# Expert rows scaled by the gate and added to the output by accumulating indirect DMA, without a combining stage

## The reference

```python
h = layernorm(x) @ Wr1 + br1;  h = gelu(layernorm(h) * ln_scale + ln_bias)
p = softmax(h @ Wr2 + br2);  top2, idx = top_k(p, 2);  gate = top2 / sum(top2)
for e in range(8):
    x1, x2 = split(layernorm(x) @ W1[e] + b1[e])       # 128 -> 2 x 512
    y = (x1 * gelu(x2)) @ W2[e] + b2[e]                # 512 -> 128
    output += y * gate_of(e)                            # 0 where e is not among the two
return x + output
```

## Time and profile before

| | us |
|---|---|
| median of three runs | 1981.48 (1976.96 to 1983.18) |
| the profiled execution | 1981.65 |
| its span, first to last instruction | 1979.9 |

### The profile page before, as it was taken

How to read it: one execution, slowest core, us unless ns; L and a number is a source line. 1 busy time by engine, 2 the same in 40 slices (tenths; PEclk the granted TensorE clock), 3 DMA queues, 4 the chain that set the end, 5 groups by cost and what they waited for, 6 DMA issues and landing times. The chain is left out here.

```text
span 1979.9 us, 50794 instructions
## 1 busy us (share of the span) xinstructions
PE 1674.4 (85%) x12709; PEld 1283.0 (65%) x12710; DVE 1455.8 (74%) x5309; ACT 1068.1 (54%) x2080; POOL 1091.8 (55%) x2255
## 2 busy tenths in 40 slices
PE   3599999999999999999999999835444699999990
PEld 1366766766766766766766766634434599999990
DVE  4588788788788788788778788736555577777775
ACT  2067666666666666666666666501111465656553
POOL 4047546547547547547547547416877455555650
PEclk8599999999999999999999999955555799999995
DMA  4436436426426427327426426274221211111119
GB/s 167 127 95 155 107 85 159 110 77 164 112 70 172 111 64 177 109 64 174 109 71 167 109 81 165 75 236 116 65 65 42 67 53 52 51 53 53 52 49 257
DMA packets 167897, 212.14 MB, mean 107 GB/s; under 512 B 28049, under 2 KB 129313, under 8 KB 167681
## 3 DMA queue, kind: packets, MB, share of 16 engines
q1 hardware_dynamic: 137216, 149.63, 27.2%
q0 software_dynamic: 30464, 59.96, 12.2%
HBM read 127.01 MB, written 77.22 MB: 103 GB/s over the span
## 5 line engine op out<-in xcount | busy, mean ns | idle before, releaser
L778 DVE CUSTOM_DVE_ANT_0 junk<-pA,lmask 128x512 bf16<-128x512 f32 x1056 | 688.2, 683 | 224.5 <-PE pA L489 114.6
L720 ACT ACTIVATE prob<-pB 128x512 f32<-128x512 f32 x512 | 305.6, 597 | 194.0 <-PE pB L510 162.9
L722 ACT ACTIVATE prob<-pB 128x512 f32<-128x512 f32 x512 | 305.2, 596 | 1.3 <-PE pB L512 1.1
L489 PE MATMUL pA<-K,QL 96*128 96x512 f32 (+3 forms) x792 | 286.1, 363 | 19.9 <-DMA K<-split_operands 14.3
L528 PE MATMUL pC<-prob,vext 128*32 128x256 f32 x4112 | 283.8, 393 | 2.9 <-POOL prob L403 2.9
L403 POOL TENSOR_TENSOR prob<-prob,upper_diag 128x128 f32<-128x128 f32 x512 | 255.0, 498 | 47.8 <-POOL prob L398 10.5
L512 PE MATMUL pB<-QL,K 97*128 97x512 f32 (+3 forms) x768 | 279.4, 364 | 0.0
L510 PE MATMUL pB<-QU,K 97*128 97x512 f32 (+3 forms) x640 | 269.7, 421 | 7.4 <-ACT prob L720 2.8
L491 PE MATMUL pA<-K,QU 96*128 96x512 f32 (+3 forms) x660 | 235.9, 359 | 12.1 <-DVE acc L778 7.2
L396 POOL MEMSET prob<- 1x1 f32 x448 | 39.5, 88 | 345.6 <-ACT prob L722 345.5
L1471 POOL DMA_INDIRECT expert_rows<-yb,dst x144 | 158.2, 1098 | 102.5 <-DVE yb L1592 74.5
(11 more groups left out here) (272 smaller groups left out, 3437.7 us busy)
## 6 DMA issues: line engine op xcount, KB each, us to landing
QL<-split_operands SPq DMA_DIRECT2D x67, 256.0 KB, 3.5
QU<-split_operands SPq DMA_DIRECT2D x67, 256.0 KB, 3.9
K<-split_operands SPq DMA_DIRECT2D x67, 256.0 KB, 3.9
xg<-routed_rows SPq DMA_DIRECT2D x76, 130.0 KB
QL<-split_operands SPq DMA_DIRECT2D x67, 128.0 KB, 3.5
QU<-split_operands SPq DMA_DIRECT2D x67, 128.0 KB, 3.7
K<-split_operands SPq DMA_DIRECT2D x67, 128.0 KB, 3.7
split_operands<-c_h POOLq DMA_DIRECT2D x16, 512.0 KB, 6.4
```

Of the source, the lines that this page charges most:

```text
L489: mm = pe.matmul(dst[:, 0:low], QL[0:KROWS, s, q], K[0:KROWS, s, k0:k0 + low], start=True, stop=True)
L720: act.activation(p[:, 0:HALF], pB[:, 0:HALF], ACT.Exp, scale=SCALE).then_inc(p_exp, 1)
L722: act.activation(p[:, HALF:S], pB[:, HALF:S], ACT.Exp, scale=SCALE).then_inc(p_exp, 1)
L778: v.tensor_tensor_reduce(junk[:, n % S1_BUFS, :], pA[n % S1_BUFS][:, :], lmask[:, at:at + HALF], 1.0, -3.0e38, ALU.add, ALU.max, acc[:, s, ...
```

## The change

- A row in `xs` has two more floats. Column E + 2 holds the gate of the token's second expert, column E + 3 the first one's gate less the second's. VectorE makes them in c2, by four small operations per batch, from an exp that ScalarE now does per batch ahead of the Gelu; GpSimd's scatters wait for them (`nb * C_N + C_N` in place of `C_IDX`). The token's number in the row now counts from S, so that it is the row of the output tensor. Padding rows are all 0, with -1 for the expert.
- x2 is written straight to the output tensor, which has nine blocks; its loads into SBUF are gone.
- In the expert loop VectorE makes the gate of each row (choose: two operations of 128 x 2 in place of one). ScalarE scales y by it, two activations of 128 x 128, a step later than y is made. GpSimd makes the destination with one operand fewer, from the loaded rows alone, and adds y to the output by indirect DMAs with `compute_op=ALU.add`.
- GpSimd issues the adds of a tile only when those of the tile before have landed (`y_out`); VectorE's reuse wait counts the same semaphore. SyncE's load waits also for the gate.
- combine_phase and its tensors are gone.

```diff
@@ routing_phase, gpsimd
-                    placed = known(po, nb * C_N + C_IDX)
+                    placed = known(po, nb * C_N + C_N)
@@ routing_phase, scalar
+                    act.wait_ge(c_dve, nb * C_N + C_DLT)
+                    act.activation(ex[:, :], dlt[:, :], ACT.Exp).then_inc(t_exp, 1)
                     gelu(nb + 1)
                     turned(nb + 3)
-            act.wait_ge(c_dve, B * C_N)
-            act.activation(ex[:, :], dlt[:, :], ACT.Exp).then_inc(t_exp, 1)
@@ routing_phase, vector, c2
                 v.tensor_copy(idx[k][:, :, :], posf[:, :, :]).then_inc(c_dve, 1)
+                v.wait_ge(t_exp, nb + 1)
+                v.tensor_scalar(gd[:, :], ex[:, :], 1.0, None, ALU.add).then_inc(c_dve, 1)
+                v.wait_ge(c_dve, at + 6)
+                v.reciprocal(gd[:, :], gd[:, :]).then_inc(c_dve, 1)
+                v.wait_ge(c_dve, at + 7)
+                v.tensor_tensor(rows[k][:, :, E + 2], ex[:, :], gd[:, :], ALU.mult).then_inc(c_dve, 1)
+                v.wait_ge(c_dve, at + 8)
+                v.tensor_tensor(rows[k][:, :, E + 3], gd[:, :], rows[k][:, :, E + 2], ALU.subtract).then_inc(c_dve, 1)
@@ expert_phase, gpsimd
                 for a in range(HALVES):
                     at = k * HALVES + a
-                    last = po.tensor_scalar(dst[k][:, a:a + 1], other[k][:, a:a + 1], xg[k][:, a, E:E + 1], pad_slot[:, at:at + 1], ALU.add, ALU.min)
+                    last = po.tensor_scalar(dst[k][:, a:a + 1], xg[k][:, a, E:E + 1], pad_slot[:, at:at + 1], None, ALU.max)
                 last.then_inc(places, 1)
 
             def step(it, k):
                 i = it * TURNS + k
-                place(i + 1, k + 1)
+                place(it + (k + 1) // TURNS, (k + 1) % TURNS)
                 tile = known(po, i + 1)
-                po.wait_ge(going, 2)
                 po.wait_ge(places, tile)
-                po.wait_ge(y_done, tile)
+                po.wait_ge(scaled, tile)
+                if not (isinstance(i, int) and i == 0):
+                    po.wait_ge(y_out, i * Y_N)
+                po.sem_inc(adding, 1)
                 for a in range(HALVES):
-                    po.indirect_dma_start(dram["ys"], bass.IndirectOffsetOnAxis(dst[k][:, a:a + 1], 0), yb[k][:, a, :], None).then_inc(y_out[k], 16)
+                    po.indirect_dma_start(dram["out"], bass.IndirectOffsetOnAxis(dst[k][:, a:a + 1], 0), yb[k][:, a, :], None,
+                                          compute_op=ALU.add).then_inc(y_out, 16)
@@ expert_phase, scalar
+            def scale(i, k):
+
+                act.wait_ge(y_done, i + 1)
+                for a in range(HALVES):
+                    out = act.activation(yb[k][:, a, :], yb[k][:, a, :], ACT.Copy, scale=gate[k][:, a:a + 1])
+                out.then_inc(scaled, 1)
@@
                 act.wait_ge(up_lin, i * 2 + 2)
                 weights(k, step.experts[k + 2])
+                if not (isinstance(i, int) and i == 0):
+                    scale(i - 1, (k - 1) % TURNS)
                 gelus(i + 1, k + 1, step.experts[k + 1])
                 turned(i + 2, k)
@@ expert_phase, vector
-            def slot(it, k):
-
+            def choose(it, k):
+
+                i = it * TURNS + k
                 if not (isinstance(it, int) and it == 0):
-                    v.wait_ge(y_out[k], it * (HALVES * 16))
-                v.tensor_scalar(other[k][:, :], xg[k][:, :, E + 1], keep["tile_expert"][:, bass.ds(it * TURNS + k, 1)], -float(TOKENS), ALU.is_equal, ALU.mult).then_inc(choice, 1)
+                    v.wait_ge(y_out, (i - TURNS + 1) * Y_N)
+                v.scalar_tensor_tensor(own[k][:, :], xg[k][:, :, E + 1], keep["tile_expert"][:, bass.ds(i, 1)], xg[k][:, :, E + 3],
+                                       ALU.is_equal, ALU.mult).then_inc(choice, 1)
+                v.wait_ge(choice, 2 * i + 1)
+                v.tensor_tensor(gate[k][:, :], own[k][:, :], xg[k][:, :, E + 2], ALU.add).then_inc(choice, 1)
```

More of the change, by code:

```diff
@@ L1374, in _ @@
             v.tensor_copy(keep["expert_no"][:, :], keep["tile_expert"][0:1, :]).then_inc(t_dve, 1)
-            v.wait_ge(t_exp, 1)
-            g0, g1 = keep["gate"][:, 0, :], keep["gate"][:, 1, :]
-            v.tensor_scalar(g0, ex[:, :], 1.0, None, ALU.add).then_inc(t_dve, 1)
-            v.wait_ge(t_dve, 28)
-            v.reciprocal(g0, g0).then_inc(t_dve, 1)
-            v.wait_ge(t_dve, 29)
-            v.tensor_tensor(g1, ex[:, :], g0, ALU.mult).then_inc(t_dve, 1)
-            v.wait_ge(t_dve, 30)
+            v.wait_ge(t_dve, 26)
@@ L1405, in expert_phase @@
         yb = [sb(f"yb{i}", [P, HALVES, E]) for i in range(TURNS)]
-        other, dst = [sb(f"other{i}", [P, HALVES]) for i in range(TURNS)], [sb(f"dst{i}", [P, HALVES], U32) for i in range(TURNS)]
+        own, gate = [sb(f"own{i}", [P, HALVES]) for i in range(TURNS)], [sb(f"gate{i}", [P, HALVES]) for i in range(TURNS)]
+        dst = [sb(f"dst{i}", [P, HALVES], U32) for i in range(TURNS)]
         pad_slot = sb("pad_slot", [P, TURNS * HALVES])
@@ L1414, in expert_phase @@
         w_hi, w_lo = sem("w1_high"), sem("w1_low")
-        gelu, prod, choice, places = (sem(n) for n in ("gelu_done", "product_done", "choice", "places"))
-        down, y_done, going = (sem(n) for n in ("down_done", "y_done", "going"))
-        y_out = [sem(f"y_out{i}") for i in range(TURNS)]
+        gelu, prod, choice, places = (sem(n) for n in ("gelu_done", "product_done", "gate_chosen", "places"))
+        down, y_done, going, scaled, adding = (sem(n) for n in ("down_done", "y_done", "going", "y_scaled", "tile_to_add"))
+        y_out = sem("y_added")
+        Y_N = HALVES * 16
         block = ctx.enter_context(nc.Block())
@@ L1453, in _, with place @@
         def _(po):
-            def place(i, k):
-                k, tile = k % TURNS, known(po, i + 1)
+            def place(it, k):
+                loaded = known(po, it * 16 + 16)
                 po.wait_ge(going, 2)
-                po.wait_ge(choice, tile)
+                po.wait_ge(x_in[k], loaded)
                 for a in range(HALVES):
                     at = k * HALVES + a
-                    last = po.tensor_scalar(dst[k][:, a:a + 1], other[k][:, a:a + 1], xg[k][:, a, E:E + 1], pad_slot[:, at:at + 1], ALU.add, ALU.min)
+                    last = po.tensor_scalar(dst[k][:, a:a + 1], xg[k][:, a, E:E + 1], pad_slot[:, at:at + 1], None, ALU.max)
                 last.then_inc(places, 1)
@@ L1662 @@
     dram = {k: nc.dram_tensor("in_" + k, v.shape, F32, kind="ExternalInput").ap() for k, v in arrays.items()}
-    dram["out"] = nc.dram_tensor("out", [B, S, E], F32, kind="ExternalOutput").ap()
+    dram["x2s"] = nc.dram_tensor("out", [B + 1, S, E], F32, kind="ExternalOutput").ap()
+    dram["out"] = dram["x2s"].rearrange("b s e -> (b s) e")
     dram["operands"] = nc.dram_tensor("split_operands", [2, 3, H, 4, D, S], F32).ap()
-    dram["x2s"] = nc.dram_tensor("after_attention", [B + 1, S, E], F32).ap()
     dram["xs"] = nc.dram_tensor("routed_rows", [NX * REGION, ROW], F32).ap()
-    dram["ys"] = nc.dram_tensor("expert_rows", [TOPK * TOKENS + TURNS * ROWS, E], F32).ap()
     attention_phase(nc, dram)
     with ExitStack() as ctx:
-        keep = sum_tensors(nc, ctx)
-        with ExitStack() as inner:
-            experts = {**keep, **expert_tensors(nc, inner)}
-            routing_phase(nc, dram, experts)
-            expert_phase(nc, dram, experts)
-        combine_phase(nc, dram, keep)
-    return run(nc, [{"in_" + k: v for k, v in arrays.items()}], core_ids=[0]).results[0]["out"]
+        experts = expert_tensors(nc, ctx)
+        routing_phase(nc, dram, experts)
+        expert_phase(nc, dram, experts)
+    return run(nc, [{"in_" + k: v for k, v in arrays.items()}], core_ids=[0]).results[0]["out"].reshape(B + 1, S, E)[1:]
```

109 lines of the change are left out of this document (32 added, 77 removed).

## The result

| | before | after |
|---|---|---|
| median | 1982.19 us (4 runs) | 2017.26 us (4 runs) |
| range | 1976.96 to 1983.18 us | 2009.84 to 2020.38 us |
| profiled execution | 1981.65 us, span 1979.9 | 2019.21 us, span 2017.6 |

The ratio is 1.0177 with a 95% interval of 1.0142 to 1.0211: the kernel got slower by 35 us. The forecast was 1999 us.

What follows compares the result with a forecast made beforehand. TensorE bounds the expert loop at 4.94 us a tile; a serial chain of adds at C = 5.9 would replace it. Span 1572.7 + 72C = 1997.5, so 1999 us measured, range 1944 to 2085.

Steps and rivals of the forecast that it cites:

- The last stage, removed: After the expert loop: the whole stage of 43.98 us goes, leaving about 0.5 us for the program's end.
- The chain, its shape: Expert loop: each tile's adds wait for the previous tile's landing, a chain through 72 tiles competing with TensorE's 4.94 us.
- No longer issue: Expert loop, GpSimd: an add issues like a scatter, 2.50 us per tile for two; upper bound 0.69 more, taken as none.
- Hand-over, read and packets: Expert loop, between tiles' adds: 2.5 us hand-over (1.76 to 2.62), 0.7 for reading the destination, 0.2 for packets.
- C: Expert loop: the chain's length per tile, 2.5 + 2.5 + 0.7 + 0.2 = 5.9 us, with ends 4.94 and 7.7.
- The first add: Start of the expert loop: at 1570.0 us, from 1568.98 plus 0.2 for routing and 0.8 for scaling y.
- The table loads in routing: ScalarE, exponential alternating with Gelu: 1.28 us loads hidden in idle time; the one before the first expert Gelu goes, -1.28.
- Leaving the block: After the last landing: 3.0 us to leave the expert loop's block, 4.78 less 1.82 for a landing.
- ScalarE's scaling: Expert loop: 0.61 us per tile, delaying a Gelu pair by some 0.3, nothing lost; about +0.8 once.
- The gate's operations: Expert loop, VectorE before the low half: about 0.15 us against 0.23 slack, so nothing, at most 0.1 per tile or 7 us.
- The clock: TensorE in the expert loop: a granted clock below 1.00 from its gaps would lengthen every tile; costed at nothing.
- weighed as a rival: Expert loop: an add costs little more than a scatter, 5.0 to 5.57 us per tile, 1949 us at 5.2; chance 0.25.

Runs made afterwards that it cites:

- b_wait: Kernel before, with GpSimd issuing a tile's two plain scatters only once those of the tile before have landed; 1980.71 us, ratio 0.9992.
- b_add: Kernel before, with a tile's two scatters made adds into rows filled with zeros, and nothing waiting for them; 1982.84 us, ratio 1.0013.
- b_both: Kernel before, with both the wait for the tile before and adds in place of scatters, last stage kept; 2051.56 us, ratio 1.0377.
- a_nowait: Kernel after, each of four buffers adding into its own DRAM sum, no wait for the tile before, output incomplete; 1956.41 us, ratio 0.9892.

## Why the prediction was off

The mechanism was the one forecast, and the sign. Step by step:

- **The last stage, removed: right.** 44.0 us are gone, and 4.4 us follow the last issue.
- **The chain, its shape: right.** Adds wait for landings in all 71 hand-overs, GpSimd's index work is hidden, and TensorE is released through VectorE. `b_wait`, `b_add` and `b_both` show that it takes both the wait and the add.
- **"No longer issue": the step that failed.** I priced the issue of an add as that of a scatter, 2 x 1.10 + 0.30 = 2.50, and kept 0.69 as an upper bound from the longest scatter seen. It takes 2 x 1.655 + 0.30 = 3.61. That is +1.11 us a tile for a term put at nothing, beyond that bound too. Rows that show one instruction at different times don't bound another one's.
- **Hand-over, read and packets: mis-sized the other way.** I took 2.5 + 0.7 + 0.2 = 3.4. Between two pairs there are 6.146 - 3.61 = 2.54 us. The hand-over of a plain scatter is 1.3 + 0.8 = 2.1 (`b_wait`), nearer to my lower bound of 1.76 than to the 2.5 I chose. Read and packets add 0.4, not 0.9. The 2.00 of the earlier trace rows held a loop's back edge, and I had noted it and not used it. Nor can that 2.00 agree with a fixed 2.0 us for a whole transfer, as I had it: it runs from an issue's end to the next operation, back edge included.
- **C** is 2.50 + 1.11 + 3.4 - 0.86 = 6.15 where I had 5.9. Two errors of about 1 us nearly cancelled. What is left, 0.246 x 72 = 17.7 us, is almost all of the miss. The size of C came out about right by luck; with only the first error it would have been 7.0.
- **The first add: 3.4 us late**, 1573.4 for 1570.0, which is less than the spread of routing's start. The gates came as forecast: four operations in 0.81 us (1351.52 to 1352.33) where I had 0.95. The scatter of batch 1, which I had charged with +0.95, did not wait for them. The table loads in routing are hidden, and the one ahead of the first expert Gelu is gone. But GpSimd's stall of 6 us was in no step, and routing's start, 2.4 us earlier in that execution by chance, gave part of it back.
- **Leaving the block:** 1.0 us less than in the sum. Together: +17.7 + 3.4 - 1.0 = 20.1, from 1997.5 to 2017.6.
- **ScalarE's scaling "delays nothing": right** (0.69 us, over before the next Gelu's input). **The gate's operations "nothing, at most 0.1 a tile": wrong in itself, harmless here.** They take 0.26 us a tile, which the chain covers; `a_nowait` pays it. I had counted 0.15 against a slack of 0.23. The operations delay the low half by 0.28 in the mean, for the second depends on the first (0.37 from start to start in the tile shown). And the 0.23 was no slack: in `a_nowait` TensorE again starts 0.23 after the low half is ready (1702.28 + 0.41 to 1702.92), and it is idle before that, so this is the hand-over. In the kernel before, TensorE's weight loads for y last until 1704.88 (1703.02 + 1.86) and those of the next tile start at 1704.87, 0.23 after the low half too: next to nothing was free.
- **The clock** stayed at 1.00 in the middle of the loop (1600 to 1900) in spite of TensorE's gaps of about 1 us, as I had counted on. It did not everywhere: it was 0.50, the 1.2 GHz level, from 1924 to 1926, right after TensorE had stood idle for 2.52 us, and 0.66 in the mean from 1950 to 1955. In the kernel before there is no such fall from 1600 to 1925.

```profile
1923.91 0.57 PE L1492 MATMUL pGate<-xT_h,w_h 128*128 128x256 f32 x1 [2.52 <-DVE xT_l L1569]
...
1924.00:1926.00 2.00, 2.00 (x10) 2.00 (x10) 1.17 (x2) 0.98 (x3) 1.70 (x2) 0.50 0.18 16
```

  The shares (0.83 in each of two stretches of 10 us, from 1920 and from 1950) put TensorE's loss at some 3.4 us in all, an estimate and an upper bound, since TensorE does not set the pace.

The Trainium skill ("Collectives: The Full Stack", The bandwidth ceiling), which I had weighed as a rival, puts an add's extra cost down to its second source read alone. In packets the trace agrees, 224 for an add and 112 for a scatter. In time it is far more than the 0.2 a tile that I drew from it: a link of `b_both` is longer than one of `b_wait` would be by 0.56 for the first issue and 1.0 for the later landing of the second, 1.56 in all. Of these, 2 x 0.56 = 1.12 is GpSimd's issuing, which halving the bytes shortened as little as it changed the packets. Whether the longer issue comes from the doubled packets no run here shows. Its rule of a fixed 2.0 us for such a transfer ("DMA: Bandwidth & Descriptors", Anatomy of one DMA, SWDGE path) stands near the scatter's 2.3 us to landing, and 1.3 below the add's 3.3.

## What to carry to other kernels

When each step waits for its predecessor's DMA, write down the whole link: both issues, landing, wake. Compare it with the period of the bound engine, for neither the wait nor the dearer instruction shows alone. An indirect add that waits for every predecessor cost more here than the gather and sum it replaced; waiting almost only where two tiles can meet in a row kept the gain. An engine that is hidden behind a chain must be costed again once the chain is gone.

## What was not expected of the hardware

- GpSimd takes 1.59 us (median) to issue an indirect add of 128 rows, and 1.03 to 1.06 for a scatter of the same rows. With 256-byte in place of 512-byte rows it is the same 1.59.
- From the start of its issue an add lands after 3.3 us, a scatter after 2.3.
- An add keeps the DMA engines busy for longer, and in twice the packets. The four stretches of 0.2 us from 1811.0 in the kernel after, while one add's packets run:

```profile
1811.00:1811.20 0.20, 0.20 (x4) 0.20 (x4) 0.20 (x2) 0.20 (x2) 0.04 (x1) 1.00 1.39 51
...
1811.60:1811.80 0.20, 0.20 (x4) 0.20 (x3) 0.00 (x0) 0.20 (x1) 0.00 (x0) 1.00 0.46 46
```

With 0.60 and 1.32 in the two between, their shares make 0.2 x 3.77 = 0.75 us of all 16 engines, against 0.20 for a scatter. Even so the bandwidth was never the limit: `b_add` ran at a share of 0.40.
